# Turning the rotated heads by transposing DMAs instead of TensorE, with tile rows ordered position by batch

## The reference

```python
# layer 0: a 512 x 512 weight, quantised by a codebook of 64 values per group of 128, plus a low-rank part
x = x + x @ w_eff.T
# layer 1: attention over 16 pages of 32 cached keys and over the 32 new ones; D = 128, 32 heads of q, 8 of k and v
q = rope(rmsnorm(x @ Wq.T) * q_norm_w, pos);  k = rope(rmsnorm(x @ Wk.T) * k_norm_w, pos);  v = x @ Wv.T
scores = q @ [k_cache[block_table], k].T / sqrt(D)      # cached keys past the sequence's length are masked
x = x + (softmax(scores) @ [v_cache[block_table], v]) @ Wo.T
```

## Time and profile before

| | |
|---|---|
| median of 3 runs | 2250.25 us (2249.0 to 2250.43) |
| the profiled execution | 2244.9 us |
| its span, first to last instruction | 2243.0 us |
| granted PE clock, mean | 0.989 |
| busy share PE / DVE / ACT / POOL | 96 / 77 / 65 / 56 % |
| DMA | 438 MB, mean 195 GB/s |

### The profile page before, as it was taken

One profiled execution on the slowest core, in us unless ns is written; L12 is line 12 of the kernel. 1 busy time (PEld: TensorE's weight loads), 2 busy tenths in 40 slices (PEclk: granted clock), 3 DMA queues, 4 the chain that ended last, 5 costly groups with the idle time before them and its releaser, 6 DMA issues.

```text
span 2243.0 us, 61281 instructions
## 1 busy us (share of the span) xinstructions
PE 2158.3 (96%) x18068; PEld 1411.6 (63%) x18068; DVE 1727.7 (77%) x3942; ACT 1465.5 (65%) x4967; POOL 1251.3 (56%) x2067
## 2 busy tenths in 40 slices
PE   5786989999999999999999999999999999999998
PEld 2343556666666666666666666666666666666665
DVE  6995668777777777777777777777777777777785
ACT  2542557676677776676676667667666666666664
POOL 3422126656666655665656666666656566665663
PEclk9997999999999999999999999999999999999999
DMA  3687658667667667667669667666566656666663
GB/s 103 221 279 248 222 167 238 195 193 207 200 194 207 197 191 216 203 198 211 198 191 300 179 189 238 185 177 175 175 188 181 181 173 186 183 178 177 184 178 104
DMA packets 478727, 438.06 MB, mean 195 GB/s; under 512 B 53037, under 2 KB 407676, under 8 KB 477886
## 3 DMA queue, kind: packets, MB, share of 16 engines
q1 hardware_dynamic: 433278, 295.70, 44.7%
q0 software_dynamic: 40960, 134.25, 19.6%
q10 hardware_dynamic: 4160, 4.19, 0.5%
HBM read 377.24 MB, written 56.70 MB: 193 GB/s over the span
## 4 chain that ended last, share of the span: by engine, by line
PE 84%; DVE 1%; issue 0%; ACT 0%; DVEq 0%; ACTq 0%
PE PR L1257 21%; PE Op L1238 15%; PE WOp L1296 15%; PE Sp L1204 15%; PE PTp L1215 11%; PE TRp L1270 3%; PE Sp L1207 1%; PE Op L1220 1%; PE Op L1240 1%; PE TRp L1281 1%; DVE masked L1448 0%; PE WOp L1281 0%; ACT masked L1353 0%; DVE WoT L1507 0%; DVE OT L1466 0%
## 5 line engine op out<-in xcount | busy, mean ns | idle before, releaser
L669 POOL DMA_INDIRECT pages<-values_split,rows x512 | 526.4, 1028 | 104.0 <-issue 78.5
L1347 ACT ACTIVATE pts<-PTp 128x512 f16<-128x512 f32 x512 | 305.7, 597 | 363.9 <-PE PTp L1215 363.8
L1257 PE MATMUL PR<-Wt,xT 128*128 128x512 f16 x2232 | 539.1, 380 | 0.0
L1238 PEld LDWEIGHTS Op<-pts,pages 128*128 128x128 f16 x6144 | 385.4, 98 | 121.1 <-DVE OT L1466 4.2
L1238 PE MATMUL Op<-pts,pages 128*128 128x128 f16 x6144 | 426.6, 219 | 2.4 <-DVE OT L1466 2.3
L1204 PE MATMUL Sp<-pages,qT 128*128 128x512 f16 x1536 | 416.2, 380 | 6.9 <-PEq L184 6.9
L1448 DVE CUSTOM_DVE_ANT_0 masked<-Sp,mask 128x544 f32<-128x544 f32 x512 | 370.0, 723 | 60.4 <-PE Sp L1207 54.3
L1453 DVE TENSOR_TENSOR pts<-PTp,pts 128x512 f16<-128x512 f32 x512 | 351.5, 686 | 75.1 <-ACT pts L1347 74.9
L1353 ACT ACTIVATE masked<-masked,small 128x544 f32<-128x544 f32 x512 | 379.0, 740 | 9.4 <-DVE small L1448 8.5
L1296 PE MATMUL WOp<-WoT,OT 128*128 128x512 f16 x1536 | 377.5, 379 | 0.0
L1466 DVE TENSOR_TENSOR OT<-Op,OT 128x128 f16<-128x128 f32 x512 | 148.2, 289 | 266.3 <-ACT p L1341 262.7
(11 more groups left out here) (211 smaller groups left out, 3075.5 us busy)
## 6 DMA issues: line engine op xcount, KB each, us to landing
pages<-keys_transposed SPq DMA_DIRECT2D x2048, 64.0 KB
mask<-mask_rows SPq DMA_DIRECT2D x128, 128.0 KB
v<-new_values SPq DMA_DIRECT2D x96, 128.0 KB
weights_split<-wdst SPq DMA_DIRECT2D x40, 256.0 KB
keys_transposed<-pages SPq DMA_DIRECT2D x32, 256.0 KB, 3.4
values_split<-pages SPq DMA_DIRECT2D x16, 512.0 KB, 3.6
rope_s<-rope_table SPq DMA_DIRECT2D x32, 256.0 KB
pages<-values_split,rows POOLq DMA_INDIRECT x512
```

The lines of the kernel that those rows point to most:

```text
L669: nc.gpsimd.indirect_dma_start(out=vS[:, n % 2, c, :, :].rearrange("p l n -> p (l n)"), out_offset=None, in_=v_d, in_offset=bass.IndirectO ...
L1238: nc.tensor.matmul(o, vS[:, par, c, low, h * D:(h + 1) * D], pts[:, u % 2, part, c * P:(c + 1) * P], start=(k == 0), stop=False)
L1257: m = nc.tensor.matmul(bank(k), xT[:, c, xl, :], Wp[:, c, wl, GROUP_COL[k]:GROUP_COL[k] + HID], start=(i == 0), stop=(i == NPASS - 1))
L1347: nc.scalar.activation(pts[:, u % 2, 0, :], PTp[:, :], ACT.Copy).then_inc(G.pt_hi, 1)
```

## The change

- In the long loop PE no longer turns the rotated heads (`turn_rotated` is gone there; it stays in `first_block`). ACT and DVE split qr, now in SBUF and with one buffer, into `split`: [128, ring of 2, high and rest, 512] f16. ACT then issues one DMA with transpose for each group: 128 rows x 1024 columns of f16 (256 KB) from `split` to eight blocks of 128 columns in qT or kTn. Five semaphores `heads_turned` count them; PE waits for the group's own in the tile's first slots (the keys' and the first queries' in slot 0, then one in each of slots 1, 2, 3).
- The split of a group waits for the DMA of the group two before; `rotate` waits for the split before it.
- TILE_PLAN: `split` in slots 5, 7, 10, 12, 14, `turn` (the issue, at the end of ACT's slot) in 5, 8, 12, 13, 15. Two output products move one or two slots earlier.
- Rows of a tile are position by batch (row = 4 s + b) where x, the rope table and the output of layer 0 are loaded or stored: four DMAs of 32 rows, each to every fourth partition, take the place of one. The new values are read back as whole rows of four batches.
- Scores read every fourth column of qT (stationary) and of kTn (moving).
- Gathers of cached values in places 0, 0, 1, 1. The small tables seqf, wq_b, wk_b lie in scratch space.

The diff, cut to its core:

```diff
@@ TILE_PLAN
-    turn={5: 0, 6: 1, 10: 3, 12: 4, 14: 5}, turned={6: 0, 7: 1, 11: 3, 13: 4, 15: 5},
-    wo={4: (0, 1), 7: (1, 2), 8: (2, 3), 9: (3, 4), 11: (4, 7), 12: (7, 9), 13: (9, 12), 14: (12, 14), 15: (14, 16)})
+    split={5: 0, 7: 1, 10: 3, 12: 4, 14: 5}, turn={5: 0, 8: 1, 12: 3, 13: 4, 15: 5},
+    wo={4: (0, 1), 5: (1, 2), 7: (2, 3), 9: (3, 4), 11: (4, 7), 12: (7, 9), 13: (9, 12), 14: (12, 14), 15: (14, 16)})
@@ end of the block before first_block, and the same form at x_d[t] and out_d[t - 4] inside first_block
                 for t in range(4):
-                    sp.dma_start(xin[:, t, :], x_d[t]).then_inc(G.x_first, 16)
+                    for b in range(BPT):
+                        sp.dma_start(xin[b::BPT, t, :], x_d[t, b * S:(b + 1) * S, :]).then_inc(G.x_first, 16)
@@ load_table
-            sp.dma_start(rope_s[:, :], rope_d[tile % TILES]).then_inc(G.table_loaded, 16)
+            for b in range(BPT):
+                sp.dma_start(rope_s[b::BPT, :], rope_d[tile % TILES, b * S:(b + 1) * S, :]).then_inc(G.table_loaded, 16)
@@ tile_block
+                def turned_heads(nt, k):
                     if k == 0:
+                        return kTn[:, nt, :, :].rearrange("p l (r n) -> p (l r) n", r=REP)
+                    return qT[:, nt, NORMED.index(k) - 1, :, :].rearrange("p l (r n) -> p (l r) n", r=REP)
@@ scores
-                        if u % UPT == 0 and u > 0:
-                            pe.wait_ge(G.tr_lo, len(NORMED) * (u // UPT))
-                        q0 = (h * BPT + b) * P
+                        if b == 0 and u >= UPT:
+                            if h == 0:
+                                pe.wait_ge(heads_turned[0], 16 * (u // UPT))
+                            pe.wait_ge(heads_turned[h + 1], 16 * (u // UPT))
+                        q = [qT[:, tt, h, part, b::BPT] for part in range(2)]
@@ PE's slot
-                        if ti in proj and sl in plan["turn"]:
-                            turn_rotated(ti, plan["turn"][sl], sl)
@@ ACT
+                    def rotated_high(ti, k):
+                        m_ = norm_no(ti, k)
+                        a.wait_ge(G.rope_done, m_ + 1)
+                        if m_ >= 2:
+                            before, kb = divmod(m_ - 2, len(NORMED))
+                            a.wait_ge(heads_turned[kb], 16 * (before + 1))
+                        nc.scalar.activation(split[:, m_ % 2, 0, :], qr[:, :], ACT.Copy).then_inc(G.split_high, 1)
+                    def turn_heads(ti, k):
+                        m_ = norm_no(ti, k)
+                        a.wait_ge(G.split_low, m_ + 1)
+                        a.dma_start(turned_heads((ti + 1) % 2, k), split[:, m_ % 2, :, :].rearrange("p l n -> p (l n)"), transpose=True).then_inc(heads_turned[NORMED.index(k)], 16)
@@ DVE, rotate and rotated_low
-                        if m_ >= 2:
-                            v.wait_ge(G.tr_done, m_ - 1)
                         if m_ >= 1:
-                            v.wait_ge(G.rope_done, m_)
+                            v.wait_ge(G.split_low, m_)
...
+                    def rotated_low(ti, k):
+                        m_ = norm_no(ti, k)
+                        v.wait_ge(G.split_high, m_ + 1)
+                        V.tensor_tensor(split[:, m_ % 2, 1, :], qr[:, :], split[:, m_ % 2, 0, :], ALU.subtract).then_inc(G.split_low, 1)
@@ POOL
-                            for c in ((0, 1), (2,), (3,), ())[place]:
+                            for c in ((0, 1), (2, 3), (), ())[place]:
```

More of the change, by code:

```diff
@@ L129, in build @@
         qn = sb("qn", [P, 2, HID], F32)
-        qr = sb("qr", [P, 2, HID], F32)
+        qr = sb("qr", [P, HID], F32)
+        split = sb("split", [P, 2, 2, HID], F16)
         rs_ = sb("rs_", [P, HID], F32)
@@ L214, in build @@
         cmp64 = scr[:, 3200:3264]
+        seqf, wq_b, wk_b = scr[:, 3264:3328], scr[:, 3328:3456], scr[:, 3456:3584]
         base = tiny[:, 0:1]
@@ L702, in load_new_values @@
             for place, part in enumerate((0, 1, 0)):
-                sp.dma_start(v5[place * S:(place + 1) * S, tile % 2, :, :], vn_d[tile % 2, part].rearrange("(b p) n -> p b n", b=BPT)).then_inc(v5_loaded[tile % 2], 16)
+                sp.dma_start(v5[place * S:(place + 1) * S, tile % 2, :, :], vn_d[tile % 2, part].rearrange("(p b) n -> p b n", b=BPT)).then_inc(v5_loaded[tile % 2], 16)
         def load_xT(sp, tile):
@@ L802, in _ @@
                             load_xT(sp, 1)
-                    for done in x1_stored + xT_stored:
-                        sp.wait_ge(done, 16 * TPS // 2)
+                    for done, parts in zip(x1_stored + xT_stored, (BPT, BPT, 1, 1)):
+                        sp.wait_ge(done, 16 * parts * TPS // 2)
                     sp.wait_ge(G.numbers_loaded, 32)
@@ L1079, in pieces_before @@
                 return sum(g < slot for g in piece_at)
-            def turns_before(slot):
-                return sum(UPT * t + sl < slot for t in proj for sl in plan["turn"])
             def unit(u):
@@ L1410, in _ @@
                             new_probs(s - 3)
-                        if ti in proj and sl in plan["turned"]:
-                            rotated_high(ti, tt, plan["turned"][sl])
+                        if ti in proj and sl in plan["split"]:
+                            rotated_high(ti, plan["split"][sl])
                         if s - 1 in piece_at:
@@ L1424, in _ @@
                                 new_values(ti, tt)
+                            if sl in plan["turn"]:
+                                turn_heads(ti, plan["turn"][sl])
                     for s in range(NU, NU + FLUSH):
@@ L1516, in _ @@
                         if ti in proj:
-                            if sl in plan["turned"]:
-                                rotated_low(ti, tt, plan["turned"][sl])
+                            if sl in plan["split"]:
+                                rotated_low(ti, plan["split"][sl])
                             if sl == plan["values_low"]:
```

84 lines of the change are left out of this document (27 added, 57 removed).

## The result

The changed kernel takes **2315.57 us** (median of 4 runs, 2304.65 to 2328.66) against 2249.62 for the kernel before on the same chip: ratio **1.0298** (95% interval 1.0244 to 1.0352). It is slower by some 66 us; forecast were 2194, and a range that ended at 2308. The profiled execution took 2304.65 us, its span is 2302.8, so 59.8 more than the span of before.

The account below looks back on a forecast made before the run. TensorE was taken to bound the kernel from 340 us to the end. Turning removed, -68.2, plus 5.3, 4.1 and 2 at the start gave -56.8 from 2250.25, say 2194 us; range 2174 to 2308.

Parts of the forecast that it names:

- Turning removed: Long loop, 31 tiles: 155 groups of head transposes leave TensorE at 0.44 us each, all on the path, -68.2 us.
- Split in place of evacuation, new order, moved products and gathers: Long loop: splits from SBUF replace PSUM evacuations at about equal size, and reordered work keeps its number, 0.
- Issue: ACT's queue, long loop: each transposing DMA holds it 0.5 us, hidden, with room up to 3.2 us, cost 0.
- Landing: Split of slot 14 after the slot 12 issue: DMA lands in 4 to 5 us, room 7.2, cost 0.
- Rival 3: Slot 14's split: turned heads land late, at 11 us costing 50 us, 2312 with the start; chance 0.14.
- DMA load: Long loop: five 256 KB transfers a tile raise the DMA engines' share from 0.70 to about 0.80, room remaining.
- Rotary table: Long loop: the table's three further issues (1.3 us) fall to an SP with free time in the batch, 0.
- Strided operands: Score products reading every fourth column: 0 taken, bounds +42 ns a load or 109 us in all.
- Start: Before and in the first block, each load of x becomes four: +5.3, +4.1 and +2 us, 11.4 together.
- 0.58: Whole kernel: chance that the gain is kept, 2194 us, own range 2175 to 2205.
- signs of being wrong: Whole kernel: PE's busy share in a tile below 98%, or a start costing more than 15 us.

Follow-up runs that it names:

- no_heads_moved: Changed kernel with the transposing transfers replaced by plain copies, of 16 elements a row and half after the first tile, so heads go unturned: 2217.17 us, ratio 0.9877.
- small_transposes: Changed kernel with each heads' transfer transposing only one 128 by 128 block (32 KB) from the second tile on: 38 us over no_heads_second, longest execution 2285.19.
- no_heads_second: The kernel of no_heads_moved run again, on the chip of the last group: 2239.46 us.
- turn_slot11: Changed kernel with the fourth heads' transfer issued in slot 11 instead of 12: 2279.44 us, ratio 1.0141; one run on another chip 2304.68.
- changed_second: The changed kernel itself, unaltered, run again on the chip of no_heads_second: transposing transfers cost 78 us there.
- half_transposed: Changed kernel with only the upper halves of the turned heads transferred (128 KB for 256) from the second tile on: 2266.27 us, ratio 1.0070.
- three_edits: Changed kernel with the slot 12 transfer in slot 11, the table load ahead of the page loads, and single transfers for x, x1 and table: 2239.77 us, ratio 0.9956.
- layout_only: Kernel before with only the new row order, four transfers each and strided operands, heads still turned by TensorE: 2276.34 us, ratio 1.0143.
- plain_copies: Changed kernel with plain copies of the same 256 KB instead of transposing transfers, heads not turned: 2223.47 us, ratio 0.9902.
- one_transfer_only: Changed kernel with x, x1 and the rotary table loaded by one transfer each instead of four: 2287.70 us, ratio 1.0152.

## Why the prediction failed, step by step

- **Turning removed, -68.2.** Right: 2.2 us in each tile (61.4 to 59.2), 31 times. Rows of one slot and a count of groups were enough, because PE had been busy without a gap.
- **Split in place of evacuation, new order, moved products and gathers, 0.** Right in undisturbed tiles, which are 59.2 and 57.9 us in no_heads_moved; ACT's split takes 656 ns, DVE's 691. Some 9 us come back in three tiles there.
- **Issue, 0.5 us and hidden.** Size wrong, 1.25 us (up to 2.5 in single cases). A plain one on ACT's queue has 0.47 (256 KB) and 0.60 (16 elements a row). At 1.25 it stays under the 3.2 us of room in the sum of loads. But 38 us separate small_transposes from no_heads_second, and the step had 0. How much of them is the issue, I can't show. The estimate of 1.7 us by the Trainium skill (DMA: Bandwidth & Descriptors, "Why a DMA increments its semaphore by 16 and not by 1") was nearer than my 0.5, and POOL's 1.03, my upper row, nearer still. It goes by the number of blocks alone, and the runs show a large fixed part: 1.11 us for 32 KB, 1.21 for 128, 1.25 for 256.
- **Landing, 4 to 5 us, no wait, cost 0.** This is the step that failed. The place was right, the split in slot 14, and slot 15 lost 51.7 us there; turn_slot11, with one number of the plan changed, takes all but 0.9 of it away. The room was too wide: I took 7.2 us, and the split's turn comes 6.4 us after the issue, slot 15 growing once the landing passes about 6.5. And the landing was far off: in slot 12 8.7 us in the median of the first half and 6.8 in the second. Two errors add up. A plain copy at that place lands in 6.2 to 6.4, whatever its size, though idle-time rows say 2.3 and 3.4; it is issued as sixteen page loads go out. And the transposition adds 2.3 (1.4 in changed_second), by 1056 packets of 30 ns each (13.6% less 0.5% of 16 x 2303 us, over 163680): 31 us of one engine, 1.95 of all sixteen, where I had put 0.9. Rival 3 had just this packet sum, 2.4 us, and I gave it 0.14. The Trainium skill (VectorE: DVE Perf Modes, "The three transpose paths") led to an estimate of 10.5 us; the measured landings, 6.0 to 11.8, lie mostly below it. My reading of it, eight blocks one after the other, does not hold here: in slot 8 one block lands in 4.4 to 5.1 us (small_transposes), four in 5.5 to 6.1 (half_transposed) and eight in 5.6 to 6.8 (three_edits), so most of a transfer is a fixed part and its traffic.
- **The clock, in no step.** I priced a stop of PE at its own length. Behind most of the longer ones the granted clock was 0.50, for an estimated 19 us more than before in tiles 0 to 30. Rival 3's price, what the landing exceeds 7.2 us by, had neither this nor the narrower room: at 11.8 us it says 4.6, and slot 15 grew by 8.0. That its 2312 lies near the measured 2316 is luck: it assumed 11 us in every tile, a start of 11.4 and no wait on the table.
- **DMA load, to 0.80.** Wrong for the same reason: 0.94 in the window at 1022. The sum had the bytes right and the packets not. SP's queue, with the same bytes, went from 37 to 43 ns a packet. The sixteen issues of a batch's page loads went from 9.0 us in the median to 9.5, with 13.9 at the longest; no_heads_second has 9.4 and changed_second 9.6, so little of this is the transposition's.
- **Rotary table, 0.** Wrong, and in no rival: behind sixteen page loads and with three further issues it misses the rotation of slot 4. None of these does it alone. The waits on the table are 1.1 us in layout_only, 6.7 in no_heads_moved, 16.4 in plain_copies and 23.1 in the changed kernel, and 10.0 there with single issues (one_transfer_only). The step looked at SP's free time in a batch and not at the moment at which the table is needed. It cost little while slot 15 stalled (slot 4 +13.1) and 53 us when it didn't.
- **Strided operands, 0.** 9 us, below every bound but zero: 0.02 us in a slot, with loads of 114 and 116 ns where the earlier trace rows has 97. The Trainium skill (SBUF — State Buffer, "Door 1") would have the full rate for two hits in a 16-byte line, which steps of 8 bytes have; the loads are some 18% longer, so the trace doesn't agree. The spacing of PE hides most of it, 3 ns a load being left.
- **Start, +11.4.** +23.0 in the trace, 19.7 by the layout alone. The count of issues was right; each takes 0.63 us, not the 0.44 of the earlier trace rows: 193.89 to 203.95 for sixteen, 8.3 us more than for four where I had 5.3. In a step of the first block eight of them take 5.0 us where two took 0.8, and the load of Wv goes out at 238.98, 17.9 us later and not 5.8. The other 3.3 us of the 23.0 come with the rest of the change (2.9 in no_heads_moved); from which part is open.
- **The chances.** 0.58 stood on four hidden costs that all had to be nothing; two of them (landing, table) draw on one resource, the DMA engines, whose load I had understated. They were not independent, and slower had to have more than 0.25. Both of my signs of being wrong came: the start cost 23.0 us, and PE's busy share was 88% in tile 3 and below 98% in 16 of the tiles 0 to 30.

The sum by its parts, measured where a run has them (us, in the changed kernel's span): turning -68.2, strided operands +9.6, start +23.0, last tile +4.6, stalls of the loop +90.8 as the remainder, of which slot 15 and 4 have 51.1 and 8.4 against no_heads_moved: **+59.8**. Of the 90.8, PE's longer idle time in tiles 0 to 30 is 62.4 and the lower clock an estimated 18.7; the other 9.7 I can't place.

## What to carry to other kernels

Price a DMA by its packets and by what else is in flight at the moment of its issue, not by a quiet row with the same bytes; transposing within SBUF took 1056 packets for 256 KB here, a copy 144. Before work goes to a DMA, list every buffer with its due time (who waits, how long after the issue) and give the tightest a slot more: one number in a plan took 66 us of waits away, one moved load 52 of 62. Waits are not the gain: the first was worth 31 us on one chip and 11 in the one run on another. A stop of the busiest engine is dearer than its length where the clock falls behind it, so read the granted clock in short windows and not in one of 60 us. When a stall goes, look at the next one at once, since the first had been covering for it. And where several transfers each touch every fourth partition, try a single one whose other side does the stepping: 13 us at the start here.

## What the runs showed of the hardware

- A transposing DMA within SBUF holds its queue 1.11 to 1.25 us whether it moves 32 or 256 KB, and lands, issued in slot 8, in 4.4 to 5.1 us (32 KB), 5.5 to 6.1 (128 KB) and 5.6 to 6.8 us (256 KB) beside this kernel's traffic: mostly a fixed part. The place counts as much: in slot 12 of the first half a copy of 16 elements a row lands in 6.2.
- Five of the smallest a tile cost 38 us over plain copies of 16 elements. The way is open: the issue on ACT, ACT's unnamed idle time (37 us to 128, but 41 with full transfers) and the later table come together, and no run here parts them.
- After stops of PE of 2.1 to 5.4 us the granted clock was 0.50, and six products of 1.46 us took 2.77.
- An issue to every fourth partition takes 0.63 us from one start to the next, to all in order 0.45 (0.33 to 0.45 in the first block); a single one with its DRAM rows out of order also 0.63.
- Chips differ by more than the kernel before shows: 5.9 us on it, 22.3 on the version without heads, half of it in slot 9, in which ACT is idle until something that the profile doesn't name. What that is stays open. A variant is to be compared with its neighbour on one chip.
